# Layer norms begun in the block in front of them, and block barriers without GpSimd's drain, in a four-layer network on one Trainium2 core

## The reference

```
x = x + conv_l(layer_norm(x, eps=1e-6))
x = x + ffn_l(layer_norm(x, eps=1e-5))
```

## Time and profile before

| | us |
|---|---|
| three runs | 1870.38, 1872.83, 1875.67 |
| their median | 1872.83 |
| the profiled execution | 1870.68 |
| its span, first to last instruction | 1868.5 |
| TensorE's mean granted clock | 0.963 of 2.4 GHz |

### The profile page before, as it was taken

How to read it: one execution, slowest core, us unless ns; L and a number is a source line. 1 busy time by engine, 2 the same in 40 slices (tenths; PEclk the granted TensorE clock), 3 DMA queues, 4 the chain that set the end, 5 groups by cost and what they waited for, 6 DMA issues and landing times. The chain is left out here.

```text
span 1868.5 us, 31745 instructions
## 1 busy us (share of the span) xinstructions
PE 1686.5 (90%) x11879; PEld 947.2 (51%) x11879; DVE 1100.9 (59%) x1526; ACT 977.6 (52%) x1426; POOL 879.3 (47%) x736
## 2 busy tenths in 40 slices
PE   6879999998579999877999977999999759999998
PEld 2635555554234444333444434777777525555554
DVE  5667777765863432365344245656656466777765
ACT  3454555554136666516666643666666445455554
POOL 1418877776024333312333335333333008778777
PEclk8989999999799999999999988999999979999999
DMA  5014333334102322301222230000000004333333
GB/s 119 1 24 104 114 105 108 109 107 129 29 1 77 88 81 78 84 1 28 88 80 66 91 93 1 2 1 2 1 2 1 3 1 116 110 112 122 112 113 98
DMA packets 71584, 121.43 MB, mean 65 GB/s; under 512 B 16962, under 2 KB 18690, under 8 KB 70786
## 3 DMA queue, kind: packets, MB, share of 16 engines
q1 hardware_dynamic: 71426, 119.32, 21.8%
HBM read 115.60 MB, written 3.67 MB: 64 GB/s over the span
## 5 line engine op out<-in xcount | busy, mean ns | idle before, releaser
L675 POOL TENSOR_TENSOR x<-x,mx_gated 128x512 f32<-128x512 f32 x256 | 331.4, 1295 | 94.2 <-DVE mx_gated L630 92.8
L623 DVE TENSOR_TENSOR mx_hidden<-mx_second,mx_hidden 128x1024 f32<-128x1024 f32 (+1 forms) x256 | 245.0, 957 | 179.0 <-PE mx_second L502 179.0
L778 ACT ACTIVATE mx_hidden<-mx_first,w_bias 128x1024 f32<-128x1024 f32 x256 | 264.5, 1115 | 124.8 <-PE mx_first L502 124.8
L821 POOL TENSOR_TENSOR x<-x,mx_gated 128x512 f32<-128x512 f32 x128 | 164.6, 1286 | 260.4 <-DVE mx_gated L795 260.4
L795 DVE SCALAR_TENSOR_TENSOR mx_gated<-mx_out,w_bias,mx_gates 128x512 f32<-128x512 f32 x128 | 96.0, 750 | 286.7 <-PE mx_out L752 265.3
L607 ACT ACTIVATE mx_hidden<-mx_first 128x1024 f32<-128x1024 f32 x256 | 248.6, 1022 | 18.6 <-PE mx_first L502 4.5
L571 PE MATMUL mx_out<-mx_hidden,w_second 128*64 128x512 f32 x1024 | 249.3, 606 | 5.6 <-issue 3.8
L1761 DVE TENSOR_TENSOR c_near_weights<-c_near_hats 128x768 f32<-128x768 f32 x192 | 190.0, 1037 | 103.1 <-PE c_near_turned L1632 103.0
L502 PE MATMUL mx_first<-tokens_high,w_high 64*128 64x512 f32 x1024 | 217.4, 420 | 21.6 <-PEq L64 21.3
L752 PE MATMUL mx_out<-mx_hidden,w_second 128*64 128x512 f32 x1024 | 233.4, 599 | 0.0
L599 ACT COPY mx_kept<-mx_second 128x512 f32<-128x512 f32 x128 | 75.3, 588 | 266.1 <-PE mx_second L502 266.1
(11 more groups left out here) (235 smaller groups left out, 2232.8 us busy)
## 6 DMA issues: line engine op xcount, KB each, us to landing
mx_gates<-gate_board SPq DMA_DIRECT2D x768, 128.0 KB, 3.1
w_first<-in_f_first SPq DMA_DIRECT2D x4, 1024.0 KB, 12.1
c_weight<-in_c_weight SPq DMA_DIRECT2D x1, 2304.0 KB
x<-in_x SPq DMA_DIRECT2D x8, 256.0 KB, 4.7
w_second<-in_f_second SPq DMA_DIRECT2D x4, 512.0 KB, 13.4
w_first<-in_f_first SPq DMA_DIRECT2D x4, 512.0 KB, 10.0
out_x<-x SPq DMA_DIRECT2D x16, 128.0 KB, 2.6
gate_board<-xn SPq DMA_DIRECT2D x16, 64.0 KB, 2.8
```

What stands on the lines that cost most here:

```text
L623: dve.tensor_tensor(own, second[:, 0:halves, :], own, ALU.mult).then_inc(s.hidden.semaphore, 1)
L675: pool.tensor_tensor(place, place, gated[:, n % GATED, :], ALU.add).then_inc(s.added.semaphore, 1)
L778: act.activation(hidden[:, n % HIDDEN, f], first[:, (n * F + f) % BLOCKS], ACT.Gelu, bias=w.bias1[:, e * F + f:e * F + f + 1]).then_inc(s. ...
L821: pool.tensor_tensor(place, place, gated[:, n % GATED, :], ALU.add).then_inc(s.added.semaphore, 1)
```

## The change

1. A class `Norm` holds the norm's steps. Its head is: the means of chunks 0 to 3 and the variances of pair 0 on TensorE; the table load, four squares, two copies and the root of pair 0 on ScalarE; two copies and the first reciprocal on VectorE. For norms 1 to 7 the head is written at the end of the block in front of the norm, with a wait for each chunk of x. Only norm 0 has it in its own block.
2. For that, PSUM is one tensor `k.ps` of 8 banks for the whole kernel, the squares have a place of their own, and `dev` and `scale` lie in `k.gate`.
3. What is left in the norm's block gets a new order on each engine.
4. In the mixtures the last add is VectorE's (`add_last`). In SwiGLU step 127 VectorE multiplies both halves, and ScalarE's copy and GpSimd's product of that step go.
6. `w_low` is signalled, and so are the first two `token_low`; ScalarE and GpSimd in a router norm and TensorE at a mixture's first step wait for them.

The diff, cut to its core:

```diff
+class Norm:
+    def __init__(self, k, turn, eps):
+        self.k, self.s, self.eps, self.turn = k, k.ln, eps, turn
+        self.chunks, self.pairs = turn * CHUNKS, turn * self.PAIRS
+        self.mean, self.var, self.wide = banks(k, 0, 4), k.ps[:, 4, :], banks(k, 5, 2)
...
+    def head_tensor(self, pe, ready, start=0, end=4):
+        for i in range(start, end):
+            ready(i)
+            self.centre(pe, i)
+            if i == 2:
+                self.variances(pe, 0)
+
+    def head_scalar(self, act):
+        act.activation(self.k.spare[:, 0:1], self.k.eps[self.eps][:], ACT.Sqrt)
+        self.square(act, 0)
+        self.square(act, 1)
+        self.keep(act, 0)
+        self.square(act, 2)
+        self.deviations(act, 0)
+        self.square(act, 3)
+        self.keep(act, 1)
+
+    def head_vector(self, dve):
+        self.centres(dve, 0)
+        self.centres(dve, 1)
+        self.scales(dve, 0)
...
-        block = ctx.enter_context(nc.Block())
+        block = ctx.enter_context(nc.Block(no_gpsimd_drain=True))
...
-            means(0)
-            means(1)
-            variances(0)
+                m.head_tensor(pe, loaded)
+            m.variances(pe, 1)
             means(2)
-            variances(1)
-            variances(2)
-            scales(0)
+            m.spreads(pe, 0)
+            m.variances(pe, 2)
             means(3)
+            m.spreads(pe, 1)
             if router:
-                variances(3)
-                scales(1)
                 route(0)
-                scales(2)
+            m.variances(pe, 3)
+            m.spreads(pe, 2)
+            if router:
                 turns(0)
                 route(1)
-                scales(3)
+            m.spreads(pe, 3)
...
-            centres(0)
-            centres(1)
-            scales(0)
-            centres(2)
-            scales(1)
-            scales(2)
-            norm(0)
-            centres(3)
-            norm(1)
-            scales(3)
+            if turn == 0:
+                m.head_vector(dve)
+            m.scales(dve, 1)
+            m.centres(dve, 2)
+            m.norm(dve, 0)
+            m.scales(dve, 2)
+            m.centres(dve, 3)
+            m.norm(dve, 1)
+            m.scales(dve, 3)
...
+    def add_last(self, dve, x, gated):
+        steps = CHUNKS * self.E
+        self.s.gated.wait(dve, steps)
+        self.s.added.wait(dve, steps - 1)
+        place = x[:, chunk(CHUNKS - 1)]
+        dve.tensor_tensor(place, place, gated, ALU.add).then_inc(self.s.added.semaphore, 1)
...
+        def ready(i):
+            s.act.wait(pe, STEPS - 1 if i < HALVES else STEPS)
+            s.added.wait(pe, E * (i + 1))
+        if following:
+            following.head_tensor(pe, ready, 0, 1)
         second_layer(STEPS - 1)
         third_layer(STEPS - 2)
+        if following:
+            following.head_tensor(pe, ready, 1, 2)
         third_layer(STEPS - 1)
+        if following:
+            following.head_tensor(pe, ready, 2, 4)
...
-        keep(STEPS - 1)
+        if following:
+            following.head_scalar(act)
...
-            halves = HALVES if n % 2 == 0 else 1
+            halves = HALVES if n % 2 == 0 or n == STEPS - 1 else 1
...
         gate(STEPS - 1)
+        gates.add_last(dve, x, gated[:, (STEPS - 1) % GATED, :])
+        if following:
+            following.head_vector(dve)
...
-            multiply(n - 1)
+            if n < STEPS:
+                multiply(n - 1)
...
-        add(STEPS - 1)
```

More of the change, by code:

```diff
@@ new lines, in wide_of, with centre, variances @@
+    def wide_of(self, n):
+        return self.wide if n < self.PAIRS - 1 else self.mean[:, 0:2, :]
+    def centre(self, pe, i):
+        k, s, n = self.k, self.s, i // 2
+        if n >= 2:
+            pe.wait_ge(s.squared, self.chunks + i - 3)
+            pe.wait_ge(s.kept if i % 2 else s.centred, self.pairs + n - 1)
+        pe.matmul(self.mean[:, i % 4, :], k.centring[:], k.x[:, chunk(i)], start=True, stop=True).then_inc(s.mean, 1)
+    def variances(self, pe, n):
+        k, s = self.k, self.s
+        pe.wait_ge(s.squared, self.chunks + 2 * n + 2)
+        if n >= 1:
+            pe.wait_ge(s.dev, self.pairs + n)
+        for q in range(4):
+            last = pe.matmul(self.var[self.quarter(q), 0:self.COLS], k.averages[:],
+                             k.square[:, (2 * n + q // 2) % 4, self.columns(q)], start=True, stop=True)
+        last.then_inc(s.var, 1)
@@ new lines, in spreads @@
+    def spreads(self, pe, n):
+        k, s = self.k, self.s
+        pe.wait_ge(s.scale, self.pairs + n + 1)
+        if n == self.PAIRS - 1:
+            pe.wait_ge(s.kept, self.pairs + n)
+            pe.wait_ge(s.centred, self.pairs + n)
+        elif n >= 1:
+            pe.wait_ge(s.normed, self.chunks + 2 * n)
+        for q in (0, 2, 1, 3):
+            last = pe.matmul(self.wide_of(n)[:, q // 2, self.columns(q)], k.spreading[half(q // 2), q % 2, :],
+                             k.scale[half(q // 2), n % 2, :], start=True, stop=True)
+        last.then_inc(s.wide, 1)
@@ L2152, in __init__ @@
         self.low = new("gt_low")
+        self.w_low = new("gt_w_low")
         self.w_high = new("gt_w_high")
```

317 lines of the change are left out of this document (157 added, 160 removed).

## The result

The changed kernel takes 1860.5 us (median of 6 runs, 1858.5 to 1862.9), the kernel before 1875.0 on the same chip (6 runs, 1870.4 to 1878.6). The ratio is 0.9922, 95% interval 0.9905 to 0.9940: faster by 14.5 us. The forecast was 1848 with a range of 1840 to 1859. So the direction is right, the gain is 9.2 us smaller than the 23.7 forecast, and the time lies just above the range, 12.5 above the forecast. The other 3.3 are the base: the forecast's sum taken from the median of 1875.0 gives 1851.3, and 1848 was set from a median of three runs and a profiled execution that both lay lower. The profiled execution took 1861.4 us with a span of 1859.6.

The account below looks back on a forecast made before the run. TensorE is busy 90% of the span, but norms are chains of hand-offs with neither engine full. Terms sum to 23.7 us: 1847.0 from the profiled 1870.7, 1849.1 from the median 1872.8; forecast 1848, range 1840 to 1859.

Parts of the forecast that it names:

- The clock: TensorE behind each norm's new barrier: a pause of about 2.5 us, with full clock counted behind it.
- TensorE runs at 1.2 GHz behind every head: First rival: half clock behind all seven heads, 1.6 us each, 11 us in all, time 1859; chance 0.20.
- Heads: Norm starts moved ahead of the barrier: gains 6.0 (mixture 0), 4.6 (mixtures 1, 2), 2.8 (group norm), 1.7 (convolutions 1, 2).
- The plain norm's 12.9: Three plain norms: 12.9 us from barrier end to norm end, 0.4 more than before.
- The router norm's 17.7: Four router norms: 17.7 us from barrier end to last logits against 15.49, so 2.2 lost.
- Convolutions: Heads behind convolutions 1 and 2: 3.9 gained minus 2.2 lost, 1.7 us each; convolution 0 gains nothing (-0.2).
- SwiGLU tail: End of mixture 3, which has no head: last add at 453.4 against 455.43 on mixture 0's times, 2.0 us gained.
- Norm 0: First norm, same block in new order: half of VectorE's about 1 us of waits after the first reciprocal, 0.5 gained.
- The barrier: Semaphore-only form at 21 places: taken as 0 gain, at most 6.3 us saved; each barrier stays at 0.3.
- the second rival: Barriers without GpSimd's drain are cheaper everywhere by 0.2: another 4 us, time 1844; chance 0.17.
- the third: Rival: the new barrier is dear at all 21 places; at 1.5 us more each, time 1880; chance 0.04.
- The fourth: Rival: the barrier behind the head gives back its gain; all seven losing 2 us more gives 1862; chance 0.09.

Follow-up runs that it names:

- e5: The changed kernel again, unchanged, on another chip with a second profile: 1859.8 us, ratio 0.9931 to the kernel before.
- e3: The changed kernel with six useless TensorE passes (keep_awake) at the end of each head but the first: 1855.6 us, ratio 0.9905 to the kernel before.
- e9: The changed kernel with each norm's first reciprocal behind the barrier and, in router norms, ScalarE's raw-product copy ahead of the casts: 1845.4 us, ratio 0.9854.
- e12: e9 with 24 TensorE passes at the end of norm 0's block and 16 instead of 8 behind the batch norm's product: 1843.3 us, ratio 0.9833.
- e6: The changed kernel with ScalarE's copy of the router's first raw products ahead of the first casts: 1853.8 us, ratio 0.9891.
- e10: e9 with the last variances ahead of the first router product on TensorE, as in the old order: 1844.1 us, ratio 0.9834.
- e2: The changed kernel with each norm's first reciprocal behind the barrier instead of ahead of it: 1852.1 us, ratio 0.9888.
- e4: The changed kernel with heads put back behind the barrier; new order, tails, signals and barriers kept: 1871.9 us, ratio 0.9993.
- e11: e9 with every barrier in the form of before (GpSimd drained): 1843.9 us, ratio 0.9841.
- e8: The changed kernel with the edits of e2 and e6, plus 24 TensorE passes ahead of the batch norm's product: 1850.5 us, ratio 0.9873.
- e1: The changed kernel with every barrier in the form of before (GpSimd drained): 1858.4 us, ratio 0.9918.

## Why the prediction was right and wrong

**The step that failed is "The clock"**, as the prediction put it: "the pause is about 2.5 us, from the last centring to the barrier, and I count full clock behind it". The pause was forecast fairly well (1.8 to 2.2 behind six heads, 3.1 behind mixture 2's) and so was its price (1.6; the runs show 1.6 to 1.7). What was wrong was to put the falls at none. The pause of 3.22 us in the earlier trace rows that cost nothing and the 3.21 in the earlier trace rows that cost 1.6 did not settle the question either way; e5 shows the same place with either outcome. What decides it in one execution no run shows; the count is 12 of 28, and 8 of 24 without norm 6. It entered the sum through the old ends as well: the trace of before has a granted clock of 0.64, 0.62 and 0.64 over the first six centring passes of norms 2, 4 and 6 (1.00 in norms 1, 3 and 5), so the terms 6.0, 4.6 and 4.6 of the mixtures each counted such a fall as gone, and in the changed kernel's trace all three are back. The rival "TensorE runs at 1.2 GHz behind every head" put all seven at 1.6 and came to 1859. Its mechanism is the one that acted, but not behind every head: that its 1859 lies so near the 1860.5 is in part luck, since the base was 3.3 low and other terms were off too. The Trainium skill, "TensorE: Matmul & The Clock Gate", section "Why this matters for your kernels", warns that idle gaps between bursts bring the engine back to the lower clock; the traces of after and e3 agree, 3.15 us against 1.98 for the same four passes, with passes in the gap as the only difference. But the warning is for longer gaps than those forecast here, so it did not say, as the prediction took it, that each of the seven norms would pay; the traces show the clock fall behind shorter ones too, in some cases.

What is missing between the two profiled executions, 14.7 us of the 23.7 (9.2 by the medians), by the traces: five norms at half clock behind the barrier, 8.2; two router norms that lost it again in the wait for the copy, 1.6; convolution 0's key matmuls (9.46 against 7.67) and query products (10.65 against 9.58), 2.9; the form of the barriers, 1.5, taken from the medians; TensorE's later start by 0.15 behind eleven barriers, 1.7. That is 15.9, and the start of the kernel gained 1.8 more than forecast, which leaves 14.1. Stages that two kernels have in common differ by up to 2 us (mixture 3 to the end takes 331.4 in the changed kernel and 333.4 in e3), so the match is no closer than that. Convolution 0 is 1.9 to 4.1 us longer in every trace of the changed family, and that is clock: its granted clock is 0.97 before and 0.91, 0.89, 0.93 and 0.86 in after, e5, e9 and e12, while VectorE's busy time in it is 38.1 to 38.2 us in all of them. One part of it can be read: before, the clock is back at full when the key matmuls start at 39.43, and in the changed kernel they start at 37.16 and the granted clock is 0.50 until 41 us. Why the query products differ stays open.

**Heads: right.** The sequence in mixture 0 was forecast to 457.55 for the reciprocal's end on the old clock; shifted by the 2.63 us by which this mixture's last regular group comes later in the changed kernel (446.54 to 449.17), that is 460.18, and it ended at 460.45. That shift is not all explained: the mixture began only 1.9 later. Where the clock stayed up the gains are the forecast's: 6.3 for mixture 0 (6.0), 4.3 for mixture 1 (4.6), 3.4 for the group norm (2.8), all in e5.

**The plain norm's 12.9: right at full clock.** In e3 the norm behind mixture 0 ends 12.9 us behind TensorE's first matmul (460.41 to 473.29) and 13.1 behind SP's first load (460.22), which was the mark the prediction named. In the changed kernel, with a fall, it is 14.5 and 14.7.

**The router norm's 17.7: right in size, wrong in what it was taken for.** Norm 3 took about 17.5 from the barrier to its last logits in the changed kernel. I followed the fourth root through route(0), the table load and the casts to the turn, wrote "keep their order", and booked the 2.2 lost as the price of the head. e6 and e10 show that 1.03 and 0.43 of it come off by reordering two lines. Besides, the wait it makes on TensorE costs clock again, 1.6 us in all in after and 3.0 in e5: this was not in the sum.

**Convolutions: wrong.** The sum had 1.7 each for convolutions 1 and 2; the traces have 1.0 and -0.7, -0.5 and -0.8. A 1.7 is of the size of one fall of the clock, and three of these four norms had one, behind the barrier (norm 5 in after) or in the wait for the copy (norms 3 and 5 in e5). In the fourth, norm 3 in after, the time from the last add to the last product fell from 20.26 to 18.75, 1.5 of the 1.7. With both cured, in e9, the two stretches gain 2.1 and 2.5, of which by e2 and e6 1.5 is theirs: so some 1 us of each term is still missing. More than half of that lies behind the norm's last product, which the term did not cover. From there to the mixture's first product it is 6.44 us before in both stretches, and 7.13 and 6.83 in e9: the barrier at the end is longer by 0.5 and 0.2 to TensorE, and the last logits come 0.2 later.

**SwiGLU tail: right.** 2.0 forecast; 1.90 in mixture 0 of e4, 1.9 and 1.8 from mixture 3 to the end in after and e5. That last stretch moves by up to 2 us in other traces, so the 1.90 is the better reading.

**Norm 0: 0.5 forecast, 1.3 to 2.7 measured** from the start to the first key matmul, over the traces of all kernels with the new order and no passes there. The first reciprocal already comes 1.1 to 2.2 us earlier: TensorE now has the first pair's variances ahead of the fourth mean, which takes 0.86 at this point. I had costed only the waits behind that reciprocal. The other part varies from trace to trace. The kernel as a whole does not get this gain: the start and convolution 0 together gain nothing in e11 and lose 0.4 to 2.3 us in the others (more in e8), for the clock in convolution 0.

**The barrier: no gain, as taken.** Its form has a small price, 0.06 to 0.07 at most places, 1.5 in all. My upper bound of 6.3 us gained and the second rival fall; so does the third, a dear barrier. The fourth, that the barrier behind the head gives back what the head gained, acted in small: the reciprocal ahead of the barrier cost some 3 us in seven norms (e2), the clock apart.

**The loads: nothing, as forecast. The signals: perhaps not nothing.** Convolution 1 shows no wait for a load in either trace; its first matmul waits for VectorE, until 483.06 before and 481.79 in the changed kernel, so the cover was larger than the 0.9 us of the forecast. No step of a mixture waits for w_low or token_low to be made, but TensorE's first product there starts 0.15 later behind the barrier (e1), which may be the two added waits themselves.

## What to carry to other kernels

A piece of work moved ahead of a barrier should be the piece that other engines can go on from while the barrier passes, and nothing that makes them wait for it: here the squares and sums belonged in front, and the 1.75 us reciprocal that only VectorE was busy with belonged behind, where it fills VectorE's own wait. When an order of operations is rewritten, follow every small operation that another engine waits for (a 0.36 us copy) back through its own engine's queue, for there it can stand behind work that nobody waits for. And a pause on TensorE has a price in expectation: at about 2 us of pause one time in three in this kernel, at 1.6 us each, so forecast it as a share of the cases and not as yes or no.

## What the runs showed of the hardware

The granted clock's fall behind a pause is not decided by the pause's length alone. The clock has two levels here, a granted clock of 1.00 (2.4 GHz) and of 0.50 (1.2 GHz). Behind 0.6 to 0.9 us (e3; 1.8 in its norm 6) and 1.6 us (the kernels with a late reciprocal, without norm 6) it never fell, in 7 and 42 cases; behind 1.8 to 2.2 us it fell in 8 of 24; behind 2.5 to 3.1 us (norm 6) in all eleven. The kernel before has it both ways at 3.2 (norm 2 fell, norms 3 and 5 did not). A second profile of an unchanged kernel was needed to see this, and it moved single stages by 3 us while the total moved by 4.5.

A barrier that leaves GpSimd undrained is not shorter here than one that drains it, but longer by 0.06 to 0.07 us (0.54 against 0.48 to TensorE), at one place by 0.35. And in the old form too TensorE starts 0.15 us later than before wherever its first instruction behind the barrier has two waits in front of it in the program: 0.48 in e1 against 0.33 in a norm, 0.46 against 0.31 at the start of a mixture, while VectorE has 0.31 in both. The waits are the likely cause; no run takes them out alone.
